# Short convolutions behind plain projections: taps on ScalarE and VectorE instead of in the weights

## The reference, cut to what matters

```
def dwconv_causal(x_cl, w):                      # each channel by itself, 4 taps, to the past
    k = w.shape[1]
    xp = jnp.pad(x_cl, ((0, 0), (0, 0), (k - 1, 0)))
    return conv_general_dilated(xp, w[:, None, :], (1,), 'VALID', ..., feature_group_count=x_cl.shape[1])

def short_conv_silu(x_bld, w):
    y = dwconv_causal(jnp.swapaxes(x_bld, 1, 2), w)
    return silu(jnp.swapaxes(y, 1, 2))

q = short_conv_silu(hidden_states @ Wq, conv_q_w)       # Wq, Wk, Wv: 128 x 128
k = short_conv_silu(hidden_states @ Wk, conv_k_w)
v = short_conv_silu(hidden_states @ Wv, conv_v_w)
beta = jax.nn.sigmoid(hidden_states @ Wb)
delta_out, _ = delta_rule_chunkwise(q, k, v, beta)      # chunks of 32 tokens, a 32 x 32 inverse per chunk and head
ms_out = multiscale_conv(v, ms_w3, ms_w15, ms_w31, kernel_mix_w, channel_mixer_w)
# gates from the means of these and the input choose among ms_out, delta_out and v; then a norm and @ Wo
```

## Time and profile before

| | us |
|---|---|
| median of 3 runs | 1090.07 |
| lowest and highest | 1081.75, 1095.02 |
| profiled execution | 1089.7 |
| its span, first to last instruction | 1087.7 |
| PE busy | 863.6 (79%) |
| PE's weight loads busy | 757.2 (70%) |
| DVE busy | 565.6 (52%) |
| POOL busy | 444.3 (41%) |
| ACT busy | 338.6 (31%) |

### The profile page before, as it was taken

One profiled execution on the slowest core, in us unless ns is written; L12 is line 12 of the kernel. 1 busy time (PEld: TensorE's weight loads), 2 busy tenths in 40 slices (PEclk: granted clock), 3 DMA queues, 4 the chain that ended last, 5 costly groups with the idle time before them and its releaser, 6 DMA issues. The chain is left out here.

```text
span 1087.7 us, 27167 instructions
## 1 busy us (share of the span) xinstructions
PE 863.6 (79%) x11563; PEld 757.2 (70%) x11563; DVE 565.6 (52%) x1663; ACT 338.6 (31%) x648; POOL 444.3 (41%) x550
## 2 busy tenths in 40 slices
PE   3518998989819779997999899979752599999990
PEld 3408998989707556775777667766542499999990
DVE  6615556545346953575467334823252355455546
ACT  2204443434214121343234323410231343344430
POOL 1666896344533002840084237523502223333342
PEclk9999998999959989999999999988655699999995
DMA  8723552432130000000000000000100433333336
GB/s 275 288 90 99 151 157 77 145 100 84 38 97 23 1 8 18 2 1 33 3 3 1 19 27 3 1 18 27 40 1 17 123 102 108 108 104 101 122 107 167
DMA packets 66547, 78.51 MB, mean 72 GB/s; under 512 B 8752, under 2 KB 52704, under 8 KB 65402
## 3 DMA queue, kind: packets, MB, share of 16 engines
q1 hardware_dynamic: 57466, 60.03, 18.0%
q0 software_dynamic: 8960, 16.74, 4.8%
HBM read 47.92 MB, written 30.52 MB: 72 GB/s over the span
## 5 line engine op out<-in xcount | busy, mean ns | idle before, releaser
L747 DVE TENSOR_TENSOR e_hid<-e_sg,e_pu 128x320 f32<-128x320 f32 x256 | 123.9, 486 | 193.1 <-ACT e_sg L683 98.3
L255 POOL DMA_INDIRECT queue<-xn,slot x128 | 126.6, 989 | 228.9 <-PE a_pc L1172 67.8
L266 POOL DMA_INDIRECT token<-e_rows,e_token x120 | 117.3, 977 | 172.3 <-DVE e_rows L713 140.3
L683 ACT ACTIVATE e_sg<-e_pg 128x320 f32<-128x320 f32 x256 | 111.7, 438 | 229.5 <-PE e_pg L640 134.4
L638 PE MATMUL e_pg<-e_xlo,e_whi 128*128 128x320 f32 x256 | 97.9, 382 | 19.2 <-DVE e_hid L747 11.6
L611 PE MATMUL e_po<-expert,e_hid 128*128 128x128 f32 x640 | 85.1, 277 | 0.0
L1066 PE MATMUL a_pz<-a_vhi,lag_hi 128*128 128x512 f32 x184 | 79.4, 431 | 2.5 <-DVE a_vlo L1448 2.5
L611 PEld LDWEIGHTS e_po<-expert,e_hid 128*128 128x128 f32 x640 | 81.2, 193 | 0.1
L639 PE MATMUL e_pg<-e_xhi,e_wlo 128*128 128x320 f32 x256 | 80.6, 315 | 0.0
L639 PE MATMUL e_pu<-e_xhi,e_wlo 128*128 128x320 f32 x256 | 80.4, 314 | 0.0
L640 PE MATMUL e_pu<-e_xhi,e_whi 128*128 128x320 f32 x256 | 80.4, 314 | 0.0
(11 more groups left out here) (297 smaller groups left out, 1880.3 us busy)
## 6 DMA issues: line engine op xcount, KB each, us to landing
e_xs<-queue SPq DMA_DIRECT2D x32, 322.5 KB
expert<-wexp_in SPq DMA_DIRECT2D x14, 512.0 KB
e_expert<-wexp_in SPq DMA_DIRECT2D x14, 512.0 KB
queue<-r_zero SPq DMA_DIRECT2D x4, 1290.0 KB, 10.3
token<-r_zero SPq DMA_DIRECT2D x4, 1024.0 KB
expert<-wexp_in SPq DMA_DIRECT2D x14, 256.0 KB
e_expert<-wexp_in SPq DMA_DIRECT2D x14, 256.0 KB
xn<-token SPq DMA_DIRECT2D x7, 512.0 KB
```

Of the source, the lines that this page charges most:

```text
L255: pool.indirect_dma_start(io.queue[c], bass.IndirectOffsetOnAxis(ap=k.slot[:, j, c:c + 1], axis=0), k.xn[:, j, :], None, bounds_check=SLOT ...
L266: pool.indirect_dma_start(io.token[c], bass.IndirectOffsetOnAxis(ap=token, axis=0), src, None, bounds_check=NTOK - 1, oob_is_err=False).th ...
L683: act.activation(sg[n % 2][:], pg[n % 2][:, 0:HALF], ACT.Silu).then_inc(silued, 1)
L747: dve.tensor_tensor(hid[q % 2][:, f, c * HALF:c * HALF + HALF], sg[n % 2][:], pu[n % 2][:, 0:HALF], ALU.mult).then_inc(hidden, 1)
```

## The change

The weights are no longer multiplied by the taps. PE forms the plain projection of a unit in 3 matmuls. ACT copies it from the bank into a buffer `acc`, scaled by the last tap (`first_tap`). DVE adds the other three taps, each from the same bank shifted by 1, 2 or 3 columns, with one operation each (`convolve`), every one waiting for the one before. ACT applies silu to `acc`. PE may use the bank again when DVE is done (`convolved`), where it waited for silu before. Betas stay as they were.

The values of a group behind the first use bank 0 for both halves. The zero columns of `xhi` and `xlo` and their fills go. The taps are loaded as 12 columns instead of one row spread over 128 partitions (768 KB); POOL's `fold_taps` and `split_taps` become a cast and a subtraction of the plain weights.

The lists of the three engines change with it: the large matmuls sit in other slots, gram goes from slots 6 to 9 to slots 8 to 11, routing's transposes from slots 1 and 2 to 3 and 4, its scores from 4 to 5, its counts from 8 to 9. On DVE the masks and `factors` come one chunk later, `combine`, `statistics` and `normalise` of the group after next are spread over the stage, and `low_values` stands behind the chunks. On ACT silu of the first half of the values stands ahead of `keep_means`.

```diff
+            def project(a, which, b, bank, term):
+                x, w = ((xhi, k.proj_hi), (xlo, k.proj_hi), (xhi, k.proj_lo))[term]
+                mm = pe.matmul(pz[:, bank, :].rearrange("p (s l) -> p s l", s=2), w[:, which * D:which * D + D],
+                               x[a % 2][:, 2 * b:2 * b + 2, :], start=(term == 0), stop=(term == TERMS - 1))
+                if term == TERMS - 1:
                     mm.then_inc(projected, 1)
...
-                    if behind_it and f in (1, 2):
-                        route_turn(r, f - 1)
+                    if behind_it and f in (3, 4):
+                        route_turn(r, f - 3)
...
-                    if behind_it and f == 4:
+                    if behind_it and f == 5:
                         route_score(r)
-                    if behind_it and f == 8:
+                    if behind_it and f == 9:
                         route_count(r)
-                    if ahead and f in (6, 7, 8, 9):
-                        gram(a, f - 6)
-                    if ahead and f in (5, 10):
-                        lengths(a, f // 5 - 1)
+                    if ahead and f in (8, 9, 10, 11):
+                        gram(a, f - 8)
+                    if ahead and f in (8, 9):
+                        lengths(a, f - 8)
...
-            KEYS_AT = (12, 8, 12, 8, 14)
-            SCALES_AT = (0, 0, 0, 0, 0, 8, 7, 7, 7, 7, 8, 8, 8, 9)
+            KEYS_AT = (6, 0, 0, 6, 6)
+            SCALES_AT = (0, 0, 0, 0, 0, 0, 8, 8, 8, 9, 9, 9, 9, 9)
...
-            VALUES_AT = (0, 0, 0, 0, 0, 0, 0, 0, 0, 0, 0, 0, 0, 0, 12, 12)
-            VALUES_FIRST = (0, 0, 0, 0, 0, 0, 8, 8, 8)
+            VALUES_AT = (0, 0, 0, 0, 0, 0, 0, 0, 0, 0, 0, 3, 0, 3)
+            VALUES_FIRST = (0, 0, 0, 0, 0, 3, 3)
...
+            def convolve(a, which, b):
+                unit = (2, 0, 4)[which] + b
+                z = pz[:, b if unit < 4 or not a else 0, :].rearrange("p (s l) -> p s l", s=2)
+                dve.wait_ge(tapped, UNITS * a + unit + 1)
+                for lag in range(1, TAPS):
+                    at = which * TAPS + TAPS - 1 - lag
+                    last = dve.scalar_tensor_tensor(acc[b][:, :, lag:], z[:, :, 0:SEQ - lag], k.taps[:, at:at + 1],
+                                                    acc[b][:, :, lag:], ALU.mult, ALU.add)
+                    if lag < TAPS - 1:
+                        link(last)
+                last.then_inc(convolved, 1)
...
+            def first_tap(a, which, b):
+                unit = (2, 0, 4)[which] + b
+                at = which * TAPS + TAPS - 1
+                act.wait_ge(projected, UNITS * a + unit + 1)
+                act.activation(acc[b][:].rearrange("p s l -> p (s l)"), pz[:, b if unit < 4 or not a else 0, :], ACT.Copy,
+                               scale=k.taps[:, at:at + 1]).then_inc(tapped, 1)
```

More of the change, by code:

```diff
@@ L1673, in odd @@
                 ahead, here, past, later = a < NGRP, g >= 0, r >= 0, g + 2 < NGRP
-                if past and n == 0:
+                if ahead and n == 0:
+                    convolve(a, 1, 0)
+                if past and n == 1:
                     normalise(r, rmv, rstd1, rrstd, rrooted, rnormed)
@@ L1677, in odd @@
                     cross_keys(a)
-                if later and n == 1:
-                    statistics(g + 2, mv, varied)
                 if here and n == 2:
                     keep_w(g, 1)
-                if past and n == 2:
-                    pick(r)
                 if ahead and n == 2:
+                    convolve(a, 0, 0)
                     betas(a)
                 if ahead and n == 3:
+                    if not here:
+                        convolve(a, 2, 0)
+                    weights(a)
+                if past and n == 3:
+                    pick(r)
+                if ahead and n == 4:
                     mask(a, 1)
                     if not here:
-                        normalise(g + 2, mv, std, rstd, rooted, normed, GRP // 2, GRP)
-                if past and n == 3:
-                    one_hot(r)
-                if ahead and n == 4:
+                        normalise(g + 2, mv, std, rstd, rooted, normed, 0, GRP // 2)
+                if here and n == 4:
+                    cross_outputs(2 * g)
+                if ahead and n == 5:
                     mask(a, 3)
                     factors(a)
-                if ahead and not here and n == 4:
+                    query_lengths(a)
+                if ahead and not here and n == 5:
                     low_values(a, 0)
@@ L1710, in odd @@
                     low_means(2 * g)
-                if ahead and here and n == 7:
-                    low_values(a, 0)
+                if later and here and n == 7:
+                    if past:
+                        combine(g + 2, 0)
+                    statistics(g + 2, mv, varied)
             def stage(g):
@@ L1953, in stage @@
                     keep_far(2 * g + 1)
+                if ahead and here:
+                    first_tap(a, 2, 0)
+                if here:
                     keep_values(g, 0)
                     keep_values(g, 1)
+                if ahead and here:
+                    first_tap(a, 2, 1)
+                if here:
                     keep_near(2 * g + 1)
-                    keep_means(2 * g)
-                if ahead:
+                if ahead and here:
                     silu_values(a, 0)
                 if here:
+                    keep_means(2 * g)
                     keep_scales(2 * g + 1)
-                if ahead:
+                if ahead and here:
                     silu_values(a, 1)
-                if ahead and not here:
-                    measure(a)
                 if here:
@@ L1978, in stage @@
                     power(2 * g + 1)
+                if later and here:
+                    root_rows(g + 2)
+                if here:
                     root_mix(2 * g)
@@ L1990, in stage @@
                     keep_mixture(2 * g + 1)
-            act.wait_ge(padded, 1)
+            act.wait_ge(chain, 1)
             root_rows(0)
```

194 lines of the change are left out of this document (104 added, 90 removed).

## The result

The changed kernel takes 1096.99 us (median of 20 runs, 1087.27 to 1100.85), the kernel before 1088.41 in as many (1081.75 to 1095.02): a ratio of 1.0077, with a 95% interval of 1.0060 to 1.0094. So it is 8.6 us slower, where 31 us faster was forecast, and within 2%. Its profiled execution took 1087.27 us, the shortest of its 20, and that of before 1089.7. The profiled pair therefore hides the loss in its totals: attention is 4.4 us longer in it (502.1 against 497.7, from the first statistics to the last addition), and the rest of the program 6.8 shorter. So I read pieces of it.

The account below looks back on a forecast made before the run. PE's queue was taken to bound attention's middle stages. First stage +1.3, stages 0 to 2 -10.3, -8.1 and -11.7, last stage -2: together -30.8 us from 1089.7, so 1059, in a range of 1042 to 1086.

Parts of the forecast that it names:

- PE's queue sets the middle stages: Attention's middle stages, 0 to 2: PE issues nearly all the time; its removed matmuls cap the gain at 51 us.
- First stage: Attention's first stage: 12.9 us more DVE work, inversion some 2.7 later, 1.4 saved later; net +1.3, bounds -1 and +9.
- The new work fills these gaps: First stage, before DVE's transpose: added convolutions go into DVE's 10.5 idle us of 28.1, so inversion starts only 2.7 later.
- A: Middle stages, from PE's first state update to DVE's transpose that starts the inversion: -1 us each, bounds -6 and +9.
- B: Middle stages, from A's end until DVE picks up POOL's inverse: -5.5, -3.3 and -8.3 us in stages 0 to 2.
- C: Middle stages, from B's end to the next stage's first update: -3.8, -3.8 and -2.4 us in stages 0 to 2.
- The sign that I named for it: In the profile after: C near 8.5 us, with PE waiting at the solve for the inverse's transpose.
- Last stage: Attention's last stage: moving route_turn to slots 3 and 4 takes a 3.1 us wait off PE; -2, bounds -3 and +3.
- Convolution: DVE's three linked operations per unit: 0.69 us each, 12.9 us per stage, in a line 72 times.
- Rival 1: Only PE counts: DVE's work fits its idle time and every removed matmul returns, 51 us, so 1039; chance 0.13.
- Rival 2: Half clock in A: PE's thinned slots run large matmuls at half clock, +6.7 us in three stages, 1079; chance 0.22.
- Rival 3: DVE in the chain of chunks: +8.6 us in A of three stages, first stage +2.7, 1118, slower; chance 0.08.

Follow-up runs that it names:

- b_three: Kernel before with the projections of the first three taps left out, 3 matmuls a unit instead of 12, order unchanged: 20 us faster than the kernel before.
- a_no_dve: Changed kernel without DVE's three convolution operations per unit, all else as in the changed kernel: 15 us off the changed kernel by the medians.
- b_plain: Kernel before, unchanged, profiled on the second chip: its profiled execution took 1047.25 us, 7 more than its median.
- a_plain: Changed kernel, unchanged, profiled on the second chip: 1.0091 of the kernel before, median 1050.78 us.
- a_fold0_gram: Changed kernel with the first stage taken back to the kernel before's and the Gram products one slot earlier in stages 0 to 2: 0.9950 of the kernel before.
- a_best: a_fold0_gram with stage 1's second combine moved from chunk 7 to chunk 4 and the statistics behind chunk 5: 1035.64 us, 0.9932 of the kernel before.
- a_ballast: Changed kernel with 104 added matmuls whose results nobody reads, 4 in each thinned slot: slower than the changed kernel by 10.7 us (medians) or 7 (ratios).
- a_gram: Changed kernel with Gram products and lengths one slot earlier in stages 0 to 2, masks half a chunk earlier: 3 us faster than the changed kernel.
- b_six: Kernel before with the projections of the first two taps left out, 6 matmuls a unit instead of 12: 11 us faster than the kernel before.

## Why the prediction was wrong

The forecast was 1059 us, 3% faster, in a range of 1042 to 1086; 1097 is slower than its upper end. By its own steps, with the change on the first and on the second chip:

- **"PE's queue sets the middle stages"** is the step that failed first. From PE's 92 to 94% busy time I took every removed microsecond as gained until another engine came last. b_three, with nothing added anywhere, got 20 of 51, and some 32 once the routing's steps were moved; the rest stays unexplained. PE was full partly because fillers had been laid over waits. I had listed only waits that showed; the 3.1 before route_turn in the last stage was one of them, and the same step waits 4.5 in A1 when the fillers go.
- **First stage, forecast +1.3.** The transpose is 10.9 later and the stage as much longer; on the second chip it is 8.8 longer. "The new work fills these gaps" failed: the 10.5 idle us of DVE lie between links of one chain of keys, queries and Gram, and each convolution is a link in it (7.1 us by a_no_dve). My upper bound of +9 was about the value. I also missed the Square behind `lengths` (8.5 us of hole, 2.8 of time).
- **A, forecast -1 each.** +3.0, +2.8, +5.8; on the second chip +4.3, +0.8, +4.6 (the +0.8 against a b_plain with its pause). DVE's operations are 1.6 to 3.5 of it, and by the rows of A2 above half clock can be some 3 of it there. The front of A did get shorter: a_plain runs through chunks 0 to 2 in 20.3, 26.5 and 26.3 us against 26.4, 35.7 and 31.4. The back did not: with Gram, lengths and eight or nine matmuls of the scales in each slot, PE takes 9.5 and 9.2 us for chunks 4 and 5 of stage 0, where the kernel before takes 7.8 and 6.9. I had costed the extra chunk step that falls into A at 1.5 beside its large matmuls.
- **B, forecast -5.5, -3.3, -8.3.** -2.6, +1.1, -4.3, and -2.6, +0.9, -4.1. Stages 0 and 2 have half of it. In stages 0 and 1 I had DVE come last, with its 4.3 us of convolutions in the sum; a_no_dve takes them out and B0 stays 46.6. PE waits 3.5 for the second step of the means in each stage. I put 0.7 there, silu alone, where ACT does a table load, silu and a copy first, 2.5 us. In stage 1 the moved combine took 5.75 us, not 2.2, and the outputs' transpose stood behind it. The Trainium skill, "SBUF — State Buffer", section "SBUF: two separate sides", says of a port pair that DVE and GpSimd share that two inputs in SBUF let DVE lock it against POOL operations that read SBUF, and that the one who comes second is blocked; by that rule the combine slows during POOL's inversion, and the trace agrees, 800 against 343 ns each. I had weighed it and priced it at 3 us of sum; between the profiles of a_fold0_gram and a_best B1 differs by 5.8, with its queue, and the medians by 1.5.
- **C, forecast -3.8, -3.8, -2.4.** -2.1, -3.0, -0.3, and -2.4, -3.3, +0.7: right in kind in stages 0 and 1 and too large, and nothing of it in stage 2. The sign that I named for it did not come: in no middle stage does PE wait for the inverse's transpose at the solve.
- **Last stage, forecast -2.** -7.0 and -4.3: the right way, but not shown to be the change's. The wait before route_turn went from 3.1 to 1.7 us only, and the same code's last stage differs by 6.6 between kernels.
- **Convolution, forecast 0.69.** 72 operations at 745 ns, 53.6 us busy, no issue.

Rival 1 is refuted by b_three. The measured 1097 lies between rivals 2 (1079) and 3 (1118), and each had a part. Rival 2 had the half clock right as a fact (0.84 to 0.93 in A) and by the rows of A2 as a cost, at +6.7 a stage where A grew by 0.8 to 5.8 from all causes; a_ballast shows only that adding work doesn't win it back. It isn't what lost the first stage: at 0.67 a_no_dve is within 2 us of b_plain there. Rival 3 put the operations of A at 8.6 us a stage, and they cost 1.6 to 3.5 there and 7.1 in the first stage, which it gave 2.7. No case had the new order itself losing. With the first taps it is 13 us (a_no_dve against b_three), and the moves of a_gram and a_best got 0.6% back, from 0.9988 to 0.9932.

## What to carry to other kernels

An engine at 93% whose queue carries fillers is not shown to be the bound: take its work away alone, without the replacement, before pricing the replacement. When steps move to later slots, read which single-buffered step now stands behind them, and which fillers are already in those slots. Two-input SBUF work on DVE ran 2.3 times as long beside POOL's inversion as outside it; here it belongs outside.

## What the runs showed of the hardware

- Half clock follows idle time of PE and outlasts it: in b_three 4.5 us without work and the 0.43 pitch up to 480, then a pause of 3.0 us and the same pitch up to 504, with full clock between; in b_plain the same pause and half clock to 504.4.
- PE pauses in the middle of bursts of small matmuls with nothing that it waits for: 1.08 us behind the 43rd of the 64 of the Gram above, and 3.0 in solve_keys of stage 1 in four profiles (the kernel before twice, b_three, and 3.6 in b_six) but not in h_values.
- The same kernel's last stage, on two chips, with granted clocks of 0.70 and 0.77:
```profile
713.90:813.90 100.00, 74.24 (x1394) 56.65 (x1393) 35.33 (x125) 20.91 (x32) 31.13 (x32) 0.70 0.07 23
```
```profile
695.50:778.00 82.50, 64.03 (x1394) 49.60 (x1393) 35.07 (x125) 20.91 (x32) 31.13 (x32) 0.77 0.09 28
```
